# A graph layer on one core: the change of phases written as one table of steps by time, with the returned rows fetched behind the last piece of the table

## The chip, the cores and the metric

One Trainium2 chip, one of its cores. The metric is the device time of one execution in microseconds (us), median of the runs of a kernel. The engines of the core are TensorE (PE, matmuls), VectorE (DVE), ScalarE (ACT), GpSimd (POOL, here mostly the indirect gathers) and SyncE (SP, here the issuer of most transfers). Each works through its own instructions in order and waits on semaphores for the others.

## What is computed

6250 nodes of 256 features, 100000 edges sorted by destination, 16 relation types. In short form:

```
xn  = layernorm(x)
msg = (xn @ W[rel])[src] * edge_weight            # 16 relation matrices, 256 x 256
gnn = segment_sum(msg, dst)
q, k, v = xn @ Wqkv;  k = softmax(k, over all nodes)
ctx = k^T v per head (8 heads of 32);  out = q ctx
gate = sigmoid(gelu(ln(xn) @ Wg1 + bg1) @ Wg2 + bg2)
x   = x + gnn + (out * gate) @ Wproj + bproj
t   = layernorm(x);  top-2 of 8 experts by softmax(t @ router)
x   = x + t + sum_e weight_e * (gelu(t @ w1[e] + b1[e]) @ w2[e] + b2[e])
```

Matrices are split into a high and a low part (float32r), and a product is three passes (high·high, low·high, high·low).

## The kernel before

The nodes are 49 tiles of 128 (NT), processed as 24 pairs and one tile. **Phase one** goes over all tiles: keys, values and gate inputs, and the table of the 16 relation products, which is stored to memory in four pieces a tile; k and v rows go to `kv_d`. From tile 24 (K2) on it also gathers and sums part of the edges (3 of 8 edge tiles of a row of edges) and adds the contexts of the first 24 tiles. **Phase two** goes over the pairs `i` in eight slots `s` each, and the half group S = 8i + s of edges has 3 tiles for even s and 2 for odd s (`PART`). GpSimd gathers the tiles into a ring of six half groups (`gathers`: half group S waits until S − 6 is summed), and every engine has its share of a step:

- `SELECT` (DVE) makes the matrix of destinations; `MSGS` scales the gathered rows by the edge weight. For the first pairs (`WHOLE = 2`, half groups 0 to 15) ACT scales in place and PE sums in f32, two records a tile (`L2026`); later ACT writes a high part and DVE the low part (`L1611`), and PE sums both (`L2030`, `L2031`). `SUMS` (PE) adds up in a bank, `WINDOW`/`adds` (DVE, `L1625`) adds the bank to the nodes.
- For the pair one behind (`+`): `OUT`, `GATES`, `GATE_ACT`, `GATE`, `GATE_HI`, `GATE_LOW`, `PROJ`, `STATS` (which needs the first window of the next pair), `roots2` on POOL, `MEAN`, `NORM`, `TURN`, `TURN_HI`, `TURN_LOW`, `LOGIT`, `TOP`, and the first two layers of experts.
- For the pair two behind (`-`): `LAYER1 e` (PE, then gelu `L1090` and cast `L1095` on ACT, `LOW e` on DVE), `LAYER2 e`, `ADD e`, the weights of the two experts (`WEIGHT`, `COMB`...), the bias.

The order in each slot is written out by hand in `SLOTS_OF_PAIR`; an engine takes from it the steps it has. Pair 1 has its own list, `SLOTS_OF_SECOND`. In pair 0's slots only the steps of the edges apply, and other work is put between them by conditions on `(i, s)`:

- The first rows of phase two are 4 held k and v rows (`held_contexts`), then 21 rows that come back from `kv_d` in six parts of 4 and 3 (`load_rows` on SP, `shifts` on DVE `L1540`, `exps` on ACT `L996`, `contexts` on PE `L1982`), two parts in slot 0 and one in each of the slots 1 to 4 of pair 0. The two buffers are `slot` (7 rows) and `later` (14 rows).
- Slot 5: `finish_context` (DVE), `context_turn`, `context_values`; slot 6: `head_contexts`, `query_context`, `GATES 0`; slot 7: `query_high`, `query_low`, `OUT 0`.
- The expert weights come in four chunks of 2048 columns (n = 4 to 7), each cast on ACT (`split_hi`, `L847`) and subtracted on DVE (`split_lo`, `L1186`) at the places `SPLITS` and `SPLITS_LOW`; chunk n + 2 is loaded when chunk n is split.

For pair 0 PE takes `LAYER1 0` and `LAYER1 1` in slots 5 and 6 of pair 1 and the other layers in the slots of pair 2, so all of pair 1's sums stand before `LAYER1 2` and `LAYER2 0`.

A rare branch (`far > 0`, edges too far from their window) is not entered with this input; its flag is loaded into a register (`value_load`) on POOL, DVE and PE.

Of the kernel before, what the change touches and what calls it, by code (L numbers as in the profile page):

```python
# [38 lines left out]
def gps_layer(nc, x, src, dst, rel, norm, Wr, Wqkv, Wproj, bproj, ln_g, ln_b, Wg1, bg1, Wg2, bg2,  # L39
# [14 lines left out]
    ROOTS, FIRST_ROOTS = (7, 1), (5, 0)  # L54
# [30 lines left out]
    WC = 4  # L85
    AHEAD = 2 * X
# [21 lines left out]
    with ctx:  # L108
# [62 lines left out]
        ctxbd = sb("ctxbd", [P, CC, P], F32, two)  # L171
        hgp = sb("hgp", [2 * G, 2, P], F32R, two)
        dg = sb("dg", [P, C], F32, two)
# [10 lines left out]
        ct = sb("ct", [3 * CW, 2 * P], F32R, two)  # L184

# [87 lines left out]
        half = small[:, 38:40]  # L273
        vea = small[:, 64:64 + NT - K2]
# [214 lines left out]
        def _(sp):  # L489
# [44 lines left out]

            def load_kept(k, i):
# [78 lines left out]
        def _(pool):  # L614
# [28 lines left out]
            pool.wait_ge(consts, 10)  # L643
# [196 lines left out]
        def _(act):  # L840
# [157 lines left out]
            def beside(i, s):  # L998
# [7 lines left out]
                if (i, s) == (1, 4):  # L1006
                    act.wait_ge(w_lo, 8)
# [1247 lines left out]
```

## Time and profile before

| | |
|---|---|
| median of 3 runs | 1598.66 us (1596.49 to 1599.17) |
| the profiled execution | 1598.54 us, span 1596.7 us |
| PE busy | 1563.8 us (98%), 10509 matmul records |
| DVE, ACT, POOL busy | 1339.1, 962.8, 1021.2 us |
| mean granted clock | 0.995 |

The span is the time from the first to the last instruction. Busy time of PE is modelled from pipelined matmuls, so a busy PE need not be at its peak. Phase one ends near 721 us; pair 3's slots begin at 827.85 us.

### The profile page before, as it was taken

How to read it: one execution, taken by the hardware profiler on the slowest of the kernel's cores; microseconds unless marked ns; L12 is line 12 of the kernel's file. 1: busy time of each engine (PE TensorE's matmuls, PEld its weight loads, DVE VectorE, ACT ScalarE, POOL GpSimd, SP SyncE). 2: the span in 40 equal slices, each digit the busy share in tenths (PEclk: the TensorE clock that was granted, in tenths of full speed). 3: DMA queues.
4: the chain of work that ended last, by engine and by line, in shares of the span. 5: the costliest groups of instructions: out<-in, count | busy, mean ns of one | idle time of the engine just before them, and what ended most of it. 6: DMA issues, size and time to landing. Idle time of an engine off the chain costs nothing.

```text
span 1596.7 us, 31746 instructions
## 1 busy us (share of the span) xinstructions
PE 1563.8 (98%) x10509; PEld 1439.2 (90%) x10509; DVE 1339.1 (84%) x3389; ACT 962.8 (60%) x2156; POOL 1021.2 (64%) x1111
## 2 busy tenths in 40 slices
PE   7999999999999999998799999999999999999998
PEld 6888788888888888887699999999999999999998
DVE  7888656488888888884699999999999999999985
ACT  4455322356565665654677776777677777777764
POOL 4433222677777777757687777777777777767720
PEclk9999999999999999999999999999999999999999
DMA  9776665688888889889433333343333333333320
GB/s 301 264 256 242 243 237 226 231 291 272 277 278 279 283 283 284 277 261 317 144 111 108 116 109 108 112 113 104 103 117 107 110 106 109 112 105 113 107 53 10
DMA packets 127076, 290.50 MB, mean 182 GB/s; under 512 B 21271, under 2 KB 49724, under 8 KB 126914
## 3 DMA queue, kind: packets, MB, share of 16 engines
q1 hardware_dynamic: 86068, 177.19, 30.2%
q0 software_dynamic: 39952, 110.13, 26.3%
q8 instruction: 85, 1.39, 0.4%
q10 hardware_dynamic: 894, 1.16, 0.2%
q14 instruction: 77, 0.63, 0.1%
HBM read 149.49 MB, written 138.90 MB: 181 GB/s over the span
## 4 chain that ended last, share of the span: by engine, by line
PE 94%; DMA 1%; DVE 1%; issue 1%; ACT 1%; POOL 1%; ACTq 0%; SPq 0%; DVEq 0%; POOLq 0%
PE bank L1826 74%; PE bank L2030 4%; PE bank L2031 3%; PE bank L1870 2%; PE bank L1871 2%; PE bank L1982 1%; PE bank L1881 1%; PE bank L2026 1%; POOL raw L700 1%; DMA raw<-table,idxa 1%; PE bank L2068 1%; PE bank L2080 1%; PE bank L1836 1%; DMA pad<-in_L_mix_Wg 1%; PE bank L2077 1%
## 5 line engine op out<-in xcount | busy, mean ns | idle before, releaser
L818 POOL DMA_INDIRECT stg<-table,idxcur x495 | 546.7, 1104 | 145.1 <-issue 133.1
L1826 PE MATMUL bank<-wreg,xt 128*128 128x512 f32 x2352 | 579.1, 397 | 0.2
L1826 PEld LDWEIGHTS bank<-wreg,xt 128*128 128x128 f32 x2352 | 433.4, 189 | 88.0 <-ACT stg L864 1.0
L700 POOL DMA_INDIRECT raw<-table,idxa x297 | 306.6, 1032 | 87.7 <-issue 73.7
L1826 PE MATMUL bank<-tt,wreg 128*128 128x256 f32 (+1 forms) x2400 | 324.4, 284 | 0.0
L1826 PE MATMUL bank<-wreg,ht 128*128 128x256 f32 x2352 | 313.1, 282 | 0.2 <-DVE ht L1727 0.2
L1826 PEld LDWEIGHTS bank<-tt,wreg 128*128 128x128 f32 x2400 | 300.4, 189 | 2.5
L1826 PEld LDWEIGHTS bank<-wreg,ht 128*128 128x128 f32 x2352 | 292.1, 189 | 0.4 <-DVE ht L1727 0.4
L1090 ACT ACTIVATE raw<-bank,cols 128x256 f32<-128x256 f32 (+1 forms) x400 | 164.8, 463 | 101.4 <-PE bank L1826 101.0
L1611 DVE SCALAR_TENSOR_TENSOR ml<-stg,nrm,mh 128x256 fp32r<-128x256 f32 x455 | 195.2, 478 | 13.0 <-ACT mh L1034 13.0
L1034 ACT ACTIVATE mh<-stg,nrm 128x256 fp32r<-128x256 f32 x455 | 200.8, 499 | 0.0
L889 ACT ACTIVATE mh_a<-raw,nrm 128x256 fp32r<-128x256 f32 x297 | 129.6, 500 | 118.1 <-DMA raw<-table,idxa 117.8
L1228 DVE COPY stg<-bank 128x512 f32<-128x512 f32 x196 | 134.2, 686 | 75.5 <-PE bank L1826 74.5
L1741 DVE SCALAR_TENSOR_TENSOR xres<-bank,raw,xres 128x256 f32<-128x256 f32 x392 | 169.7, 473 | 13.1 <-PE bank L1826 11.4
L864 ACT COPY stg<-bank 128x512 f32<-128x512 f32 x196 | 112.5, 581 | 101.8 <-PE bank L1826 100.2
L1361 DVE SCALAR_TENSOR_TENSOR ml_a<-raw,nrm,mh_a 128x256 fp32r<-128x256 f32 x297 | 126.7, 480 | 53.0 <-ACT mh_a L889 52.5
L1095 ACT CAST ht<-raw 128x512 fp32r<-128x512 f32 (+1 forms) x200 | 122.5, 612 | 72.4 <-PE bank L1826 67.4
L1727 DVE TENSOR_TENSOR ht<-raw,ht 128x512 fp32r<-128x512 f32 (+1 forms) x200 | 134.6, 673 | 11.7 <-ACT ht L1095 9.5
L2030 PE MATMUL bank<-mh,sel 128*128 128x256 f32 x455 | 120.3, 291 | 0.0
L2031 PE MATMUL bank<-ml,sel 128*128 128x256 f32 x455 | 117.0, 281 | 0.0
L665 POOL TENSOR_TENSOR xres<-xres,bpb 128x256 f32<-128x256 f32 x24 | 19.4, 809 | 136.0 <-DVE kvs L1215 135.5
L1594 DVE TENSOR_TENSOR sel<-dbl,dpr 128x384 fp32r<-128x384 f32 x198 | 95.0, 480 | 9.7 <-PE bank L2026 9.6
(244 smaller groups left out, 2134.8 us busy)
## 6 DMA issues: line engine op xcount, KB each, us to landing
table<-stg SPq DMA_DIRECT2D x196, 512.0 KB, 3.9
kv_d<-kvs SPq DMA_DIRECT2D x49, 256.5 KB, 5.2
xt_d<-xt SPq DMA_DIRECT2D x49, 256.0 KB, 4.7
xtp<-xt_d SPq DMA_DIRECT2D x24, 512.0 KB
stg<-table,idxcur POOLq DMA_INDIRECT x495
sk<-kv_d SPq DMA_DIRECT2D x24, 256.5 KB, 5.7
out_x<-xres SPq DMA_DIRECT2D x24, 256.0 KB
xres<-in_x POOLq DMA_DIRECT2D x23, 256.0 KB, 4.2
```

Source lines behind the costliest of these rows:

```text
L700: pool.indirect_dma_start(ring_a[:, r * EARLY + j, :], None, table[0:LIMIT, :], bass.IndirectOffsetOnAxis(ap=idxa[:, at:at + 1], axis=0)). ...
L818: pool.indirect_dma_start(stg[:, ring_at(S, j), :], None, table, bass.IndirectOffsetOnAxis(ap=idxcur[:, at:at + 1], axis=0)).then_inc(gath ...
L889: act.activation(mh_a[:, (r % 2) * EARLY + j, :], ring_a[:, r * EARLY + j, :], ACT.Copy, scale=nrm[:, bass.ds(EB * q + j, 1)]).then_inc(hi ...
L1034: act.activation(mh[:, (s % 2) * CUT + j, :], stg[:, ring_at(S, j), :], ACT.Copy, scale=nrm[:, bass.ds(at + j, 1)]).then_inc(msg_hi, 1)
L1090: act.activation(hf[e % 2][:, c * 256:c * 256 + nt * P], bank[2 + e % 2][:, c * 256:c * 256 + nt * P], ACT.Gelu, bias=b1c[:, 2 * e + c:2 * ...
L1228: dve.tensor_copy(stage[:, j // 2, (j % 2) * 512:(j % 2 + 1) * 512], bank[3 + j % 4][:]).then_inc(copied(k, j)[0], 1)
L1611: dve.scalar_tensor_tensor(out=ml[:, m, :], in0=stg[:, ring_at(S, j), :], scalar=nrm[:, bass.ds(at + j, 1)], in1=halves(mh[:, m, :]), op0= ...
L1727: dve.tensor_tensor(ht[e % 2][:, LO, :, 0:n], cols2(hf[e % 2], n), halves(ht[e % 2][:, HI, :, 0:n]), ALU.subtract).then_inc(h_lo, 1)
L1741: dve.scalar_tensor_tensor(out=xk, in0=bank[6 + e % 2][:, a * C:(a + 1) * C], scalar=comb[:, a, e:e + 1], in1=xk, op0=ALU.mult, op1=ALU.ad ...
L1826: mm = pe.matmul(dst, stat(a, c), mov(b, c), start=(n == 0), stop=(n == 3 * chunks - 1))
L2030: pe.matmul(bank[u % 2][:, 0:C], sel[:, m, :], mh[:, m, :], start=(s % 2 == 0 and j == 0), stop=False)
L2031: mm = pe.matmul(bank[u % 2][:, 0:C], sel[:, m, :], ml[:, m, :], start=False, stop=(s % 2 == 1 and j == PART[1] - 1))
```

## The change

- The change of phases (pairs 0 to 2, half groups 0 to 23) is one list, `CHANGE`, followed by every engine with `follow`; the conditions on `(i, s)` and `SLOTS_OF_SECOND` are gone, and `run` begins at pair 3.
- Parts 2 to 5 of the returned rows stand earlier among the sums. SP's loads are written as two loops with single rows; parts 0 and 1 are shifted and exponentiated ahead of the wait for the end of phase one.
- Half groups 4 to 19 are whole in place of 0 to 15 (`WHOLE_GROUPS`).
- A chunk of expert weights is cast and subtracted in two halves (`HIGH n h`, `LOW_PART n h`).
- `NORM` is divided: the second scaling of the rows is the step `KEEP`, in `CHANGE` behind `TURN_HI` for pair 0.
- A tiny gelu (`GELU_TABLE`) stands between `MSGS 0 3` and `MSGS 0 4` on ACT.
- `LAYER1 2` and `LAYER2 0` of pair 0 stand before the sums of half group 13 (they stood behind 15); the rest of pair 0's experts is spread over half groups 13 to 23.
- GpSimd: the mask of heads has four columns and is made at the start; the roots of pairs 0 and 1 come before gather (4, 0) and (5, 1) of the next pair in place of (5, 0) and (7, 1).
- PE's load of the far flag and its branch stand behind two parts of rows, DVE's behind `SHIFT 1`.
- Some small buffers have places of their own instead of in `raw`.

```diff
-    ROOTS, FIRST_ROOTS = (7, 1), (5, 0)
+    ROOTS, EARLIER_ROOTS = (7, 1), {1: (4, 0), 2: (5, 1)}
...
-            load_rows(0)
-            load_rows(1)
-            first_phase_over(sp)
-            for part in range(2, 2 * GROUPS):
-                load_rows(part)
+            sp.wait_ge(sum_a, ER)
+            for b in range(2):
+                sp.wait_ge(kv_st[b], 16 * ((KEPT + SLOTS) // 2))
+            for n in range(FREE_ROWS):
+                load_row(n // 4, n)
+            sp.wait_ge(ctx1_mm, KEPT)
+            for n in range(FREE_ROWS, SLOTS):
+                load_row(1, n)
+            first_phase_over(sp)
+            for returned in range(2, 2 * GROUPS):
+                for n in range(*span_of(returned)):
+                    load_row(returned, n)
...
-                sp.wait_ge(w_lo, n + 1)
+                sp.wait_ge(w_lo, splits_of(n, 1))
                 load_chunk(n + 2)
...
+            def HIGH(n, h):
+                act.wait_ge(raw_in[n % 2], 32 * (n // 2 - 1))
+                if n >= 6:
                     act.wait_ge(ctx_mm, HELD + REST)
+                act.copy(wreg[:, HI, place_of(n), h * CC // 2].rearrange("p r o -> p (r o)"),
+                         raw[:, n % 2, h * WC * C:(h + 1) * WC * C]).then_inc(w_hi, 1)
...
+            for ready in range(2):
+                EXP(ready)
             first_phase_over(act)
...
-                act.wait_ge(edge_mm, S - 1)
+                if S < 2:
+                    act.wait_ge(ctx_mm, HELD)
+                else:
+                    act.wait_ge(edge_mm, S - 1)
...
+            def LOW_PART(n, h):
+                dve.wait_ge(w_hi, splits_of(n, h))
+                dve.tensor_tensor(wreg[:, LO, place_of(n), h * CC // 2].rearrange("p r o -> p (r o)"),
...
+            for ready in range(2):
+                SHIFT(ready)
+            dve.wait_ge(flag_ready, 1)
+            far = dve.value_load(flag[0:1, 0:1], min_val=0, max_val=NT * P * R)
+            first_phase_over(dve)
...
-WHOLE = 2
+WHOLE_GROUPS = (4, 20)
...
+CHANGE = (
+    "HELD_ROWS", "ROWS_OF 0", "ROWS_OF 1", "FAR_EDGES", "SELECT 0 0", "SELECT 0 1", "FADE", "SHIFT 2", "EXP 2", "SHIFT 3",
+    "MSGS 0 0", "ROWS_OF 2", "EXP 3", "SUMS 0 0", "ROWS_OF 3", "SHIFT 4", "MSGS 0 1", "EXP 4", "SELECT 0 2",
+    "ROWS_OF 4", "SUMS 0 1", "SHIFT 5", "EXP 5", "SELECT 0 3", "MSGS 0 2", "ADDS 0 0", "ROWS_OF 5", "MSGS 0 3", "GELU_TABLE",
+    "SUMS 0 2", "SUMS 0 3",
+
+    "CONTEXT", "SELECT 0 4", "MSGS 0 4", "SELECT 0 5", "CONTEXT_PE", "CONTEXT_TURN", "SUMS 0 4", "HIGH 4 0", "MSGS 0 5",
+    "VALUES", "ADDS 0 1", "LOW_PART 4 0", "HEADS", "SUMS 0 5", "HIGH 4 1", "HIGH 5 0", "SELECT 0 6", "QUERY", "GATES 0 2",
+    "LOW_PART 4 1", "QUERY_ROWS", "GATE_ACT 0 2", "OUT 0 2", "MSGS 0 6", "SELECT 0 7", "ADDS 0 2", "SUMS 0 6", "GATE 0 2",
+    "GATE_HI 0 2", "MSGS 0 7", "CLEAR", "GATE_LOW 0 2", "SUMS 0 7", "PROJ 0 2", "HIGH 5 1", "SELECT 1 0", "LOW_PART 5 0",
+    "MSGS 1 0", "ADDS 0 3", "SELECT 1 1", "SUMS 1 0", "LOW_PART 5 1", "MSGS 1 1", "SUMS 1 1", "SELECT 1 2", "ADDS 1 0",
+    "HIGH 6 0", "STATS 0 2", "LOW_PART 6 0", "MSGS 1 2", "SUMS 1 2", "MEAN 0 2", "NORM 0 2", "TURN 0 2", "SELECT 1 3",
+    "TURN_HI 0 2", "TURN_LOW 0 2", "KEEP 0 2", "MSGS 1 3", "SUMS 1 3", "LAYER1 0 2 0", "SELECT 1 4", "HIGH 6 1",
+    "LOGIT 0 2", "LOW_PART 6 1", "LAYER1 0 2 1", "ADDS 1 1", "MSGS 1 4", "TOP 0 2", "LOW 0 2 0", "SUMS 1 4", "HIGH 7 0",
+
+    "WEIGHT 0 2", "SELECT 1 5", "LOW 0 2 1", "MSGS 1 5", "COMB 0 2", "COMB_HI 0 2", "LAYER1 0 2 2", "LAYER2 0 2 0", "OUT 1 2",
+    "SUMS 1 5", "GATES 1 2", "LOW_PART 7 0", "SELECT 1 6", "ADDS 1 2", "HIGH 7 1",
...
+    "ADD 0 2 5", "LOW 0 2 7", "MSGS 2 3", "BIAS2_ADD 0 2", "TURN 1 2", "TURN_HI 1 2", "LAYER2 0 2 6", "SUMS 2 3",
+    "TURN_LOW 1 2", "ADDS 2 1", "SELECT 2 4", "MSGS 2 4", "SUMS 2 4",
+
+    "ADD 0 2 6", "LAYER1 1 2 0", "LOGIT 1 2", "SELECT 2 5", "MSGS 2 5", "LAYER2 0 2 7", "LOW 1 2 0", "TOP 1 2", "SUMS 2 5",
+    "LAYER1 1 2 1", "ADDS 2 2", "ADD 0 2 7", "SELECT 2 6", "MSGS 2 6", "SUMS 2 6", "SELECT 2 7", "MSGS 2 7", "SUMS 2 7",
 )
+def follow(order, **steps):
+    for entry in order:
+        name, *numbers = entry.split()
+        if name in steps:
+            steps[name](*map(int, numbers), *((8,) if name in OF_GROUPS else ()))
...
-    for i in range(2, pairs):
+    for i in range(3, pairs):
```

## Rows read from the trace of the kernel before

**Rows 1.** The page, busy us, share and instructions of each engine.

```profile
PE 1563.8 (98%) x10509; PEld 1439.2 (90%) x10509; DVE 1339.1 (84%) x3389; ACT 962.8 (60%) x2156; POOL 1021.2 (64%) x1111
```

**Rows 2.** Busy time in two windows: PE, PEld, DVE, ACT, POOL, clock, DMA.

```profile
720.00:827.85 107.85, 91.96 (x552) 81.94 (x550) 68.71 (x158) 62.26 (x124) 79.41 (x81) 0.94 0.61 195
827.85:860.70 32.85, 32.85 (x278) 32.72 (x277) 30.98 (x87) 23.69 (x56) 25.90 (x26) 1.00 0.41 113
```

**Rows 3.** Waits of PE, 715 to 800 us: total, times, longest.

```profile
PE bank L2026 <- ACT stg L1030: 4.1, 2, 2.6
PE bank L1982 <- ACT slot L996: 3.9, 1, 3.9
PE bank L2007 <- DVE ctxbd L1761: 1.6, 1, 1.6
...
PE bank L2068 <- ACT scr L1055: 1.2, 1, 1.2
```

**Rows 4.** Windows of 2 us on PE: busy, granted clock, DMA share, GB/s.

```profile
728.00:730.00 2.00, 0.00 (x0) 0.61 1.08 316
...
734.00:736.00 2.00, 2.00 (x8) 0.68 1.05 379
...
786.00:788.00 2.00, 0.66 (x2) 0.62 0.30 76
...
792.00:794.00 2.00, 1.97 (x6) 0.68 0.45 131
```

**Rows 5.** PE's timeline: start, us, line, operation, records, idle before.

```profile
730.03 8.90 PE L1982 MATMUL bank<-slot 128*128 128x257 f32 x28 [3.94 <-ACT slot L996]
...
749.16 6.23 PE L1982 MATMUL bank<-later 128*128 128x257 f32 x28
755.23 2.32 PE L2026 MATMUL bank<-stg,sel 128*128 128x256 f32 x10
...
782.14 1.78 PE L1826 MATMUL bank<-tt,wreg 128*128 128x256 f32 x12
...
796.39 1.58 PE L1826 MATMUL bank<-wreg,ht 128*128 128x256 f32 x12
```

**Rows 6.** PE's timeline at the start of pair 3's slots.

```profile
827.85 1.60 PE L1826 MATMUL bank<-tt,wreg 128*128 128x256 f32 x12
829.29 1.59 PE L1826 MATMUL bank<-wreg,ht 128*128 128x256 f32 x12
```

**Rows 7.** DVE's timeline: shift, weight subtraction, selection, low messages, window.

```profile
727.66 1.23 DVE L1540 TENSOR_TENSOR slot<-slot,dg 128x1024 f32<-128x1024 f32 x1 [3.46 <-DMA slot<-kv_d]
...
753.35 2.37 DVE L1186 TENSOR_TENSOR wreg<-raw,wreg 128x2048 fp32r<-128x2048 f32 x1 [2.36 <-ACT wreg L847]
...
820.12 0.55 DVE L1594 TENSOR_TENSOR sel<-dbl,dpr 128x384 fp32r<-128x384 f32 x1
...
821.85 1.27 DVE L1611 SCALAR_TENSOR_TENSOR ml<-stg,nrm,mh 128x256 fp32r<-128x256 f32 x3
...
823.75 0.88 DVE L1625 TENSOR_TENSOR xres<-bank,xres 64x256 f32<-64x256 f32 x2
```

**Rows 8.** ACT's timeline: weight cast, then the first gelu and messages.

```profile
751.44 1.88 ACT L847 CAST wreg<-raw 128x2048 fp32r<-128x2048 f32 x1
...
784.00 1.28 ACT L1090 ACT_TABLE_LOAD   x1 [2.39 <-PE bank L1826]
785.29 0.84 ACT L1090 ACTIVATE raw<-bank,cols 128x256 f32<-128x256 f32 x2
786.17 0.62 ACT L1095 CAST ht<-raw 128x512 fp32r<-128x512 f32 x1
786.69 2.10 ACT L1030 ACTIVATE stg<-stg,nrm 128x256 f32<-128x256 f32 x5
```

**Rows 9.** POOL's first gather of phase two; landing of the weight chunks.

```profile
725.00 0.99 POOL L818 DMA_INDIRECT stg<-table,idxcur  x1 [1.23 <-DMA table<-stg]
...
DMA to landing us min/median/max: 3.8/9.3/14.2
```

More of the change, by code:

```diff
@@ L797, in _ @@
                     pool.wait_ge(far_x, k + 1)
+            for h in range(PIECES):
+                pool.wait_ge(tbl_st[h], 16 * NT)
             def gathers(i, groups):
@@ L1097, in slot_of @@
             def slot_of(i, s, groups, p1, n1, p2, n2):
[L1098 to L1109 removed]
+                in_slot(i, s, groups, p1, n1, p2, n2, MSGS=MSGS, GATE_ACT=GATE_ACT, GATE_HI=GATE_HI, NORM=NORM, KEEP=KEEP,
+                        TURN_HI=TURN_HI, WEIGHT=WEIGHT, COMB_HI=COMB_HI, COMBT_ACT=COMBT_ACT, LAYER1=LAYER1)
+            follow(CHANGE, EXP=EXP, HIGH=HIGH, GELU_TABLE=GELU_TABLE, QUERY_ROWS=QUERY_ROWS, MSGS=MSGS,
+                   GATE_ACT=GATE_ACT, GATE_HI=GATE_HI, NORM=NORM, KEEP=KEEP, TURN_HI=TURN_HI, WEIGHT=WEIGHT, COMB_HI=COMB_HI,
+                   COMBT_ACT=COMBT_ACT, LAYER1=LAYER1)
             run(slot_of, NP, TAIL_GROUPS)
@@ L1625, in adds, with ADDS @@
                     dve.tensor_tensor(xk, bank[u % 2][a:b, 0:C], xk, ALU.add).then_inc(edge_add, 1)
+            def ADDS(i, u, groups):
+                adds(i, u)
             def WINDOW(i, s, groups):
@@ L1958, in _ @@
             pe.wait_ge(k_shift_diag, 2)
-            pe.matmul(bank[1][:, C:2 * C], halves(ones[:]), dg[:], start=True, stop=True).then_inc(kmb_mm, 1)
-            pe.wait_ge(flag_ready, 1)
-            far = pe.value_load(flag[0:1, 0:1], min_val=0, max_val=NT * P * R)
+            pe.matmul(bank[1][:, C:2 * C], halves(ones[:]), dg, start=True, stop=True).then_inc(kmb_mm, 1)
             pe.wait_ge(add_a, ALL_ADDS)
@@ L2179 @@
     ("-ADD 2", "*SELECT", "-LOW 4", "-COMBT_ACT", "*MSGS", "+STATS", "-LAYER1 5", "+PROJ", "-LAYER2 3", "*SUMS"),
-    ("-ADD 3", "*SELECT", "-LOW 5", "*MSGS", "+MEAN", "*WINDOW", "-LAYER1 6", "+NORM", "-LAYER2 4"),
+    ("-ADD 3", "*SELECT", "-LOW 5", "*MSGS", "+MEAN", "*WINDOW", "-LAYER1 6", "+NORM", "+KEEP", "-LAYER2 4"),
     ("-ADD 4", "*SELECT", "-LOW 6", "*MSGS", "*LAST_WINDOW", "-LAYER1 7", "*SUMS 4", "+TURN", "+TURN_HI", "-LAYER2 5", "*SUMS",
@@ L2186 @@
 )
-SLOTS_OF_SECOND = (
-    ("*SELECT", "*MSGS", "*WINDOW", "+GATE", "+GATE_HI", "+GATE_LOW", "*SUMS"),
-    ("*SELECT", "*MSGS", "+PROJ", "*SUMS"),
-    ("*SELECT", "*MSGS", "*WINDOW", "+STATS", "*SUMS"),
-    ("*SELECT", "*MSGS", "+MEAN", "+NORM", "*SUMS"),
-    ("*SELECT", "*WINDOW", "+TURN", "+TURN_HI", "*MSGS", "+TURN_LOW", "*SUMS"),
-    ("*SELECT", "+LAYER1 0", "+LOGIT", "*MSGS", "*LAST_WINDOW", "+LOW 0", "*SUMS"),
-    ("*SELECT", "+TOP", "*MSGS", "*WINDOW", "+LAYER1 1", "*SUMS"),
-    ("*SELECT", "*MSGS", "*SUMS"),
-)
+OF_GROUPS = ("SELECT", "MSGS", "SUMS", "ADDS")
+CHANGE = (
+    "HELD_ROWS", "ROWS_OF 0", "ROWS_OF 1", "FAR_EDGES", "SELECT 0 0", "SELECT 0 1", "FADE", "SHIFT 2", "EXP 2", "SHIFT 3",
[26 rows of a table added]
+)
+def follow(order, **steps):
[3 more added lines that the diff above has]
+            steps[name](*map(int, numbers), *((8,) if name in OF_GROUPS else ()))
 def in_slot(i, s, groups, p1, n1, p2, n2, **steps):
-    for entry in (SLOTS_OF_SECOND if isinstance(i, int) and i == 1 else SLOTS_OF_PAIR)[s]:
+    for entry in SLOTS_OF_PAIR[s]:
         name, *expert = entry[1:].split()
```

232 lines of the change are left out of this document (92 added, 140 removed), and 9 rows, old and new, of the table CHANGE.

## The prediction

> **What bounds the kernel now.** I read the page first. TensorE (PE) is busy in 98% of the span and is nearly the whole chain that ended last [rows 1]. The list of waits by engine names no PE wait at all from 800 to 1500 us. The windows by stage say the same: from 827.85 us (the first layer-1 product of pair 3's slots) one pair of tiles takes 32.85 us, PE busy in all of it, VectorE (DVE) in 30.98, ScalarE (ACT) in 23.69 [rows 2]. So neither end of the kernel is in play, and an edit counts only by what PE loses in the change of phases, 720 to 827.85 us, where it is busy 91.96 of 107.85 us. The steps that the diff reorders all lie there.
>
> The list of PE's waits there adds up to the 15.9 us (four of its ten rows stand in [rows 3]): 3.9 for the first returned rows, then nine short ones between 757 and 787 us, each the latency of one link of pair 0's first passage (context, query, gate, projection, norm, turn, first expert). Two stretches of low clock come on top [rows 4]: granted 0.50, the lower of the two levels (1.2 GHz), after the wait at 726 and again after the one that ended at 787, each some 6.5 us. The first costs 2.7 us (28 records of returned rows in 8.90 us against 6.23 later [rows 5]). The second is full of work except 0.6 us, so it costs about 3.0.
>
> PE's work up to 827.85 is the same in both kernels: as many rows, products and message tiles. Sixteen half groups have whole (f32) messages in both; they are groups 0 to 15 before and 4 to 19 after. So I walk the new table with durations of these rows and ask when PE reaches the same place.
>
> **The walk.** Durations, start to start: a whole tile 0.43 on PE (5 in 2.16), a split tile 0.24, a returned row 0.87 (28 records are 7 rows in 6.1 [rows 5]), an expert layer 1.42 [rows 6]. On DVE a selection 0.35 to 0.47, a low message 0.42, a window 0.35 to 0.8, a weight subtraction 2.3 and so 1.15 for a half [rows 7]. On ACT a message 0.42, a gelu with its cast 1.45, an expert weight cast 1.9 and so 0.95 for a half [rows 8].
>
> Up to 738.8 nothing moves: the rows are issued at the same place behind the last store of the table, and PE's first row waits for the same landing. Then the new order puts the rows of the returned parts ahead of the sums, and of the sums only groups 0 and 1 (5 split tiles, 1.2 us) stand before the last row, where four whole half groups (10 tiles, 4.3 us) stood. The last row ends at 752.1 in place of 755.2: **3.1 earlier**.
>
> From there the chain, each end worked out from the one before: context sums on DVE 753.3 (the low messages of group 3 are ahead of them), its turn on PE 754.0, copy 755.0 (two selections ahead), VALUES 756.4, HEADS 757.1, QUERY 758.3, its two halves 759.7, OUT 761.5, the gate's three steps 763.7, PROJ 765.8, groups 8 and 9 on PE 767.9, one window 768.8, STATS 770.9 (2.1, as in the trace), roots and MEAN 772.4, NORM and TURN 774.2. KEEP is now behind TURN_HI, and halves of weights pass between, so the chain is stopped less than by the 2.3 us pieces of before. But then ACT does KEEP (1.0) and MSGS 1 3, and PE has SUMS 1 3 ahead of LAYER1 0: it starts at 777.1, where it was 782.1 [rows 5]. PE idles 1.0 at QUERY_ROWS, 1.3 elsewhere, 4.2 before TURN, 2.0 behind it.
>
> Next LAYER1 0, LOGIT, LAYER1 1 end at 781.1. The gelu table load, 1.28 us on the path at 784.0 before [rows 8], now lies near 750, where ACT waits for DVE anyway. MSGS 1 4 is behind HIGH 6 1 and two gelus, so PE idles 2.2. LAYER2 0 starts at 785.7. Before it was 796.4 [rows 5], but with groups 13 to 15 summed (7 whole tiles, 3.0) and without the dearer sums of 16 to 19 still ahead (10 tiles, 1.9): comparable is 791.5. **Lead 5.8 us** at full clock.
>
> **The clock.** A wait of 4.2 us, followed by 0.6 us of transposes and 2.0 more of waiting, is longer than either that brought the low clock before [rows 3, 4]. I expect one stretch of 6.5 us that begins between 773 and 777: 1.5 us lost if it is early, 3.3 if it holds work throughout; I take 2.3. Lead 3.5. The Trainium skill has the same picture (TensorE: Matmul & The Clock Gate, What's actually happening): throttled is the default and activity releases it; the trace agrees with 0.50 and 1.00, and by that rule, too, the wait of 4.2 us ends in the low clock.
>
> **The tail gives it back.** Pair 0's experts now run beside groups 13 to 23, eleven in place of eight, so the last four groups of pair 2 stand close together, and these have split messages. Up to the end of SUMS 2 3 PE has 28.4 us of work after 785.7 and no wait in my walk. Then:
> - SUMS 2 4 directly follows SUMS 2 3, but its low messages are behind ADDS 2 1, which waits for SUMS 2 3: 0.4 window, 0.5 selection, three messages 1.3, less 0.5 of overlap: **1.7 idle**;
> - MSGS 2 5 is behind the gelu of LAYER1 1 0: **0.4**;
> - SUMS 2 6 directly follows LAYER1 1 1, but its messages on ACT are behind that layer's gelu (1.5), then message and low message, three tiles: **2.9**;
> - SUMS 2 7 behind it: **0.7**.
> Sum 5.7. The steady slots have none of these waits: they put the messages ahead of the layer. Result: 3.5 − 5.7 = **2.2 us slower**, place for place 830 in place of 827.85. The profiled execution took 1598.54 us for its span of 1596.7, the median is 1598.66, so 1600.9. As a check by idle time: 3.9 + 2.3 + 6.2 + 2.2 + 5.7 = 20.3 after against 15.9, and a low stretch of 2.3 against 3.0: +3.7. The two ways differ by 1.5 us, the drain of a matmul counted as busy or not; that is my error in any case.
>
> **Costed at nothing, with its cover.** POOL's head mask, three short operations, goes from 722 to the start and to four columns. POOL waits for DVE's first variance there, and PE then for a DMA; at 725 POOL waited 1.2 more for the table's store [rows 9], so nothing is won either. Without cover it is that 1.2 at most. The load of the far flag and its branch move on DVE between SHIFT 1 and SHIFT 2; before they lay inside a wait of 3.46 [rows 7], which bounds them. Of the gap of 2.9 us there 1.2 is free after two selections and FADE, and EXP 2 has 1.7 more before PE asks for it. So the loss is between 0 and 0.6; I take 0. The Trainium skill prices a compare-and-branch at about 0.1 us (Advanced Engine Details and Errata, Control Flow Timing); by that the sum stays as it is, and no row here times one. PE passes its branch with matmuls queued to 738.9. Chunk 6 of the weights leaves SP after LOW_PART 4 1, at 758.7 and not 755.7. These transfers took 3.8 to 14.2 us to land [rows 9]; at 5.3 it is there at 764, needed at 767; at 14.2 it would hold MSGS 1 2 and cost 2. GpSimd's gathers, 1.25 apart, wait for group 1's sum until 749.5 now and for STATS before group 12, and still land ahead of the messages that use them. The new small buffers cost nothing: only addresses change.
>
> **Rivals.**
> 1. *The tail hides* (chance 0.18). DVE and ACT are well ahead at SUMS 2 3 and the last groups cost PE little. For it: DVE is 1 to 2 us idle in several slots of the walk. Against it: the orders above are fixed by waits, not by load. If at most 1.5 of 5.7 are lost, the kernel is faster by 2 to 5.8: 1593 to 1596.6, say 1594.9. It turns faster from the point where the tail takes less than the lead, 3.5 us.
> 2. *A second low clock in the tail* (0.27). 2.9 and 0.7 idle with 0.7 of small sums between is near what preceded the stretch at 786.8. It would run into saturated slots and cost 2 to 3.3: 1603.5.
> 3. *No low clock near 775, or the table changes little* (0.15): lead 5.8, tail 5.7: 1598.6.
> The forecast itself has 0.40.
>
> **Numbers.** Likeliest 1600.9. A measurement here can tell 0.2% (3.2 us) from no change. Faster by more than that is nearly all of rival 1: 0.18. Slower is rival 2 and a quarter of the forecast: 0.37. Within it the rest: 0.45. The range takes in rival 1's middle and rival 2 with the 2 us of a late chunk: 1594.5 to 1605.5.
>
> **What would show it.** The windows should have PE idle 19 to 21 us up to pair 3 instead of 15.9; its waits should be for ACT and DVE messages late in the table (about 2.9 once, 1.7 once) and about 4 before TURN; returned rows should end near 752; a stretch at 0.50 should begin between 773 and 777, and layer 1 of expert 0 start near 777. If the first layer of pair 3's slots starts before 825, the tail was wrong; if LAYER2 0 starts after 790, the chain was; if PE waits for a DMA of weights, the chunks were.

## The result and the profile after

| | before | after |
|---|---|---|
| median (lowest to highest) | 1598.66 us (1596.49 to 1599.18) | 1605.69 us (1602.70 to 1609.76) |
| profiled execution, its span | 1598.54, 1596.7 | 1605.69, 1604.0 |
| mean granted clock | 0.995 | 0.993 |

The ratio is 1.0051, 95% interval 1.0038 to 1.0063: slower, by 7.0 us between the medians (the ratio stands for 8.2) where 2.2 was forecast, and 0.2 us above the top of the range. These seven runs of the changed kernel lie 7 us apart and the seven of the kernel before 3, but that can't be laid to the change: 28 later runs of the kernel before lie 9 us apart.

Phase one of this execution ended a little earlier: DVE's last copy of the table starts at 719.40, before at 720.15. In the other kernels timed below, which run the same phase one but for the change, it starts anywhere from 717.02 to 721.10, so a difference of 0.75 says nothing of the change. The tables below therefore count from that copy. From it to the first layer of pair 3's slots it was 107.70 us and is now 114.81: **7.1 us**. What of that goes to waits is in the list of PE's waits of the changed kernel from 715 to 834.3 us (total, times, longest), which answers to [rows 3]:

```profile
PE bank L2083 <- ACT scr L1068: 6.4, 2, 4.9
PE bank L2039 <- ACT stg L1040: 4.9, 3, 2.2
PE bank L1995 <- ACT slot L1004: 4.8, 1, 4.8
PE bank L2043 <- DVE ml L1628: 4.7, 4, 2.6
PE bank L1841 <- DVE wqc L1795: 1.0, 1, 1.0
```

They sum to 21.8 us, where the same list summed to 15.6 from copy to pair 3 before. Many short waits have become few long ones: before no wait in the passage of pair 0 was over 2.6, now there are 4.9, 2.15 and 2.1 in a row, one of 1.5 before the second turn, and four in the tail (2.6 the longest, 4.7 together), a place where before there was none. PE's timeline of the changed kernel has each (start, duration, records, idle before), answering to [rows 5] and [rows 6]:

```profile
729.99 8.36 PE L1995 MATMUL bank<-slot 128*128 128x257 f32 x28 [4.81 <-ACT slot L1004]
...
751.33 0.47 PE L2043 MATMUL bank<-mh,sel 128*128 128x256 f32 x1
...
774.20 1.11 PE L2083 MATMUL bank<-ident,scr 128*128 128x128 f32 x4 [4.92 <-ACT scr L1068]
777.47 2.05 PE L2039 MATMUL bank<-stg,sel 128*128 128x256 f32 x4 [2.15 <-ACT stg L1040]
778.95 3.10 PE L1841 MATMUL bank<-tt,wreg 128*128 128x256 f32 x12
...
786.48 1.53 PE L2039 MATMUL bank<-stg,sel 128*128 128x256 f32 x6 [2.08 <-ACT stg L1040]
787.66 1.77 PE L1841 MATMUL bank<-tt,wreg 128*128 128x256 f32 x12
789.27 1.58 PE L1841 MATMUL bank<-wreg,ht 128*128 128x256 f32 x12
790.68 1.59 PE L1841 MATMUL bank<-xtp,wqc 128*128 128x256 f32 x12
...
817.16 0.66 PE L2083 MATMUL bank<-ident,scr 128*128 128x128 f32 x4 [1.52 <-ACT scr L1068]
...
821.59 0.36 PE L2043 MATMUL bank<-mh,sel 128*128 128x256 f32 x1 [1.47 <-DVE ml L1628]
...
831.69 0.35 PE L2043 MATMUL bank<-mh,sel 128*128 128x256 f32 x1 [2.60 <-DVE ml L1628]
...
834.21 2.62 PE L1841 MATMUL bank<-tt,wreg 128*128 128x256 f32 x12
836.67 1.57 PE L1841 MATMUL bank<-wreg,ht 128*128 128x256 f32 x12
```

The first layer of an expert takes 3.10 us at 778.95 and some 1.6 elsewhere: the clock. Its windows (2 us each: PE busy, granted clock, DMA share, GB/s), answering to [rows 4]:

```profile
770.00:772.00 2.00, 0.00 (x0) 0.92 1.09 377
...
776.00:778.00 2.00, 0.53 (x1) 0.50 0.42 125
...
780.00:782.00 2.00, 2.00 (x12) 0.52 0.40 119
...
832.00:834.00 2.00, 1.68 (x10) 0.78 0.58 169
834.00:836.00 2.00, 2.00 (x11) 0.50 0.21 66
836.00:838.00 2.00, 2.00 (x17) 0.87 0.44 131
```

So the clock is at its lower level (1.2 GHz) for some 10 us around the first turn and for some 3.4 around 834: the half microsecond from 832.50 still has 1.00, the one from 833.50 has 0.50. Behind 838 both kernels run the same slots.

One wait of the tail can be followed over two engines. ACT's timeline of the changed kernel: the messages of `SUMS 2 6` (five of `L1047`) stand behind the gelu of the layer that PE has only just finished.

```profile
829.12 0.84 ACT L1106 ACTIVATE wv<-bank,cols 128x256 f32<-128x256 f32 x2 [2.55 <-PE bank L1841]
829.99 0.62 ACT L1111 CAST ht<-wv 128x512 fp32r<-128x512 f32 x1
830.52 2.10 ACT L1047 ACTIVATE mh<-stg,nrm 128x256 fp32r<-128x256 f32 x5
```

ACT was idle 2.55 us ahead of that gelu; its list has no message in that place.

### The profile page after: what moved, and what is told of

Same layout as the page of the kernel before. It is cut to its first block, busy times and chain, and to the rows that moved or that the text cites. A ratio compares the mean times of both kernels' runs of the same rounds, so it can differ in the third digit from the quotient of the medians.

```text
span 1604.0 us, 31756 instructions
## 1 busy us (share of the span) xinstructions
PE 1563.7 (97%) x10509; PEld 1439.3 (90%) x10509; DVE 1338.9 (83%) x3393; ACT 963.3 (60%) x2161; POOL 1028.4 (64%) x1111
## 4 chain that ended last, share of the span: by engine, by line
PE 92%; POOL 2%; DMA 2%; issue 2%; ACT 1%; DVE 1%; ACTq 0%; SPq 0%; DVEq 0%; POOLq 0%
PE bank L1841 73%; PE bank L2043 4%; PE bank L2044 3%; PE bank L1885 2%; PE bank L1886 2%; POOL raw L722 2%; PE bank L1995 1%; PE bank L1896 1%; PE bank L2039 1%; DMA raw<-table,idxa 1%; PE bank L2083 1%; PE bank L2095 1%; PE bank L1851 1%; DMA pad<-in_L_mix_Wg 1%; PE bank L2092 0%
## 5 line engine op out<-in xcount | busy, mean ns | idle before, releaser
L1047 ACT ACTIVATE mh<-stg,nrm 128x256 fp32r<-128x256 f32 x455 | 200.7, 499 | 2.9 <-PE bank L2044 2.9
L1761 DVE SCALAR_TENSOR_TENSOR xres<-bank,mix,xres 128x256 f32<-128x256 f32 x392 | 169.7, 473 | 18.1 <-PE bank L1841 16.4
L1106 ACT ACTIVATE wv<-bank,cols 128x256 f32<-128x256 f32 (+1 forms) x200 | 82.4, 464 | 62.3 <-PE bank L1841 62.3
L1106 ACT ACTIVATE cd<-bank,cols 128x256 f32<-128x256 f32 (+1 forms) x200 | 82.5, 463 | 46.4 <-PE bank L1841 46.1
L1111 ACT CAST ht<-wv 128x512 fp32r<-128x512 f32 (+1 forms) x100 | 61.2, 612 | 55.7 <-PE bank L1841 53.5
```

Of the source, the lines that this page charges most:

```text
L1047: act.activation(mh[:, (s % 2) * CUT + j, :], stg[:, ring_at(S, j), :], ACT.Copy, scale=nrm[:, bass.ds(at + j, 1)]).then_inc(msg_hi, 1)
L1106: act.activation(hf[e % 2][:, c * 256:c * 256 + nt * P], bank[2 + e % 2][:, c * 256:c * 256 + nt * P], ACT.Gelu, bias=b1c[:, 2 * e + c:2 * ...
L1761: dve.scalar_tensor_tensor(out=xk, in0=bank[6 + e % 2][:, a * C:(a + 1) * C], scalar=comb[:, a, e:e + 1], in1=xk, op0=ALU.mult, op1=ALU.ad ...
```

## The experiments

Eleven kernels ran, each timed in five rounds beside the kernel before. Two numbers are given for each: the ratio to the kernel before with its 95% interval, and the distance from the last table copy to pair 3's first layer in its one profiled execution (before 107.70, after 114.81). "Low clock" is the time at the lower level within that distance, added up over windows of 1 us as (1 − granted clock) / 0.5, and "waits" is the sum of PE's waits in it.

The last two columns say how far that one execution stands for its kernel: its own time less the kernel's median, and the granted clock as the mean of all timed executions. In a span of 1600 us each 0.001 of it is 3.2 us at the lower level.

| kernel | ratio [interval] | distance | waits | low clock | profiled less median | granted clock, mean of all |
|---|---|---|---|---|---|---|
| before | 1 | 107.70 | 15.6 | 13.6 | -0.1 | 0.9950 to 0.9952 |
| after | 1.0051 [1.0038, 1.0063] | 114.81 | 21.8 | 18.1 | 0.0 | 0.9929 |
| tail order | 1.0010 [0.9999, 1.0021] | 109.91 | 17.4 | 17.1 | +2.4 | 0.9944 |
| one sum earlier | 1.0042 [1.0025, 1.0059] | 118.55 | 20.4 | 27.3 | +6.0 | 0.9921 |
| pair 2 by the old slots | 1.0020 [1.0008, 1.0033] | 116.17 | 18.9 | 30.7 | +4.0 | 0.9929 |
| dummy work at the turn | 1.0029 [1.0016, 1.0042] | 113.23 | 16.3 | 7.9 | +0.4 | 0.9961 |
| tail, norm, dummy work | 0.9993 [0.9982, 1.0005] | 105.72 | 10.5 | 6.8 | +1.9 | 0.9976 |
| before with dummy work | 0.9992 [0.9981, 1.0003] | 107.06 | 14.0 | 10.3 | +0.2 | 0.9958 |
| groups 20 to 23 whole | 1.0035 [1.0022, 1.0048] | 113.64 | 20.3 | 17.1 | +2.3 | 0.9950 |
| tail, norm, two sums earlier | 1.0005 [0.9991, 1.0019] | 108.71 | 15.1 | 17.1 | -0.4 | 0.9935 |
| tail, norm | 1.0004 [0.9991, 1.0017] | 112.50 | 16.2 | 23.9 | +3.4 | 0.9942 |
| tail, norm, dummy work twice | 0.9983 [0.9970, 0.9995] | 104.06 | 7.0 | 0.0 | +0.8 | 0.9992 |
| before with dummy work twice | 0.9987 [0.9974, 1.0000] | 108.04 | 10.9 | 10.2 | +0.3 | 0.9967 |

### The tail's order

```diff
-    "ADD 0 2 5", "LOW 0 2 7", "MSGS 2 3", "BIAS2_ADD 0 2", "TURN 1 2", "TURN_HI 1 2", "LAYER2 0 2 6", "SUMS 2 3",
-    "TURN_LOW 1 2", "ADDS 2 1", "SELECT 2 4", "MSGS 2 4", "SUMS 2 4",
...
-    "ADD 0 2 6", "LAYER1 1 2 0", "LOGIT 1 2", "SELECT 2 5", "MSGS 2 5", "LAYER2 0 2 7", "LOW 1 2 0", "TOP 1 2", "SUMS 2 5",
-    "LAYER1 1 2 1", "ADDS 2 2", "ADD 0 2 7", "SELECT 2 6", "MSGS 2 6", "SUMS 2 6", "SELECT 2 7", "MSGS 2 7", "SUMS 2 7",
+    "ADD 0 2 5", "LOW 0 2 7", "MSGS 2 3", "BIAS2_ADD 0 2", "SELECT 2 4", "MSGS 2 4", "TURN 1 2", "TURN_HI 1 2",
+    "LAYER2 0 2 6", "SUMS 2 3", "TURN_LOW 1 2", "SUMS 2 4", "ADDS 2 1",
...
+    "ADD 0 2 6", "SELECT 2 5", "MSGS 2 5", "LAYER1 1 2 0", "LOGIT 1 2", "LAYER2 0 2 7", "SUMS 2 5", "SELECT 2 6", "MSGS 2 6",
+    "SELECT 2 7", "MSGS 2 7", "LOW 1 2 0", "TOP 1 2", "LAYER1 1 2 1", "ADDS 2 2", "ADD 0 2 7", "SUMS 2 6", "SUMS 2 7",
```

> The changed kernel with one edit: the last four half groups' selections and messages stand ahead of the windows and gelus that held them (SELECT and MSGS 2 4 ahead of TURN 1, MSGS 2 5 ahead of LAYER1 1 0, MSGS 2 6 and 2 7 ahead of LAYER1 1 1); PE's order is the same. Theory A, the order in the tail: PE waited 4.7 us there (1.5, 0.3, 2.6, 0.3) and then worked about 3.4 us at the low clock, 1.9 us lost. At least 3.5 of the idle and all of the low clock go, so 4 to 6.5 us faster than the changed kernel, near 1600. Theory B, the loss is the middle (wait before TURN 0 and the long low clock there): under 1 us. Theory C, the tail is short of DVE time whatever the order: the waits move to the windows, 0 to 2 us.

1599.12 us. The waits for low messages are gone from the list (4.7 to 0), and so is the low clock around 834; the waits ahead of both turns stay at 6.4, and so does the low clock in the middle. PE's order is the same, so this is a matter of where DVE and ACT do their share. It gives back 4.9 us of distance, and 1.0 more behind it, since pair 3's first layer is at full clock again; the ratios give 6.6 us (1.0051 to 1.0010, times 1598.7). It is the largest part of the loss.

### One sum ahead of the mean

```diff
-    ... "SUMS 1 2", "MEAN 0 2", "NORM 0 2", "TURN 0 2", "SELECT 1 3", "TURN_HI 0 2", "TURN_LOW 0 2", "KEEP 0 2", "MSGS 1 3", "SUMS 1 3",
+    ... "SUMS 1 2", "SELECT 1 3", "MSGS 1 3", "SUMS 1 3", "MEAN 0 2", "NORM 0 2", "TURN 0 2", "TURN_HI 0 2", "TURN_LOW 0 2", "KEEP 0 2",
```

> The changed kernel with one edit: SELECT, MSGS and SUMS 1 3 stand ahead of MEAN 0 in place of behind KEEP 0, so half group 11 is summed in the wait for TURN 0 and LAYER1 0 follows TURN_LOW. Theory B: the 2.15 us wait behind KEEP goes, and the sum (2 us at the low clock) leaves the low stretch: LAYER1 0 starts 2.5 to 3.5 us earlier, and the kernel is faster by 2 to 3.5 us. Theory A holds beside it, and its tail waits stay as they are (4.7 us). If the gathers are late for half group 11, PE waits for ACT on a DMA there and the gain is under 1 us.

1603.5 us, no clear gain, and the profile is worse in the middle. The 4.9 us ahead of the first turn are gone (the 1.5 left is the second turn's), but others have come: 4.0 for messages and 2.1 for a selection, and the low clock lasts 20 us, 772 to 793. PE's waits in this kernel, copy to pair 3:

```profile
PE bank L2039 <- ACT stg L1040: 4.7, 2, 4.0
PE bank L2043 <- DVE ml L1628: 4.7, 4, 2.6
PE bank L2039 <- DVE sel L1611: 2.1, 1, 2.1
PE bank L2083 <- ACT scr L1068: 1.5, 1, 1.5
```

The messages were late because ACT waited for the gathered rows of that half group; its timeline in this kernel:

```profile
772.64 0.91 ACT L1040 ACTIVATE stg<-stg,nrm 128x256 f32<-128x256 f32 x2 [4.21 <-DMA stg<-table,idxcur]
```

The wait was moved, not filled: that is the last case of what was expected. The profiled execution is 6 us slower than this kernel's median, so its 20 us of low clock are more than is usual for it; the mean granted clock of all its executions (0.9921) is still the lowest of the table.

### Pair 2 by its old slots

The table ends behind `SUMS 1 7`; `run` begins at pair 2, and its roots stand before gather (7, 1).

```diff
-    for i in range(3, pairs):
+    for i in range(2, pairs):
```

> The changed kernel with the table ended behind SUMS 1 7 and pair 2 run by the old slots, its roots at gather (7, 1); all sums of pair 1 stand before LAYER1 0 2 again, as in the kernel before. Theory A (the experts' spread over half groups 13 to 23 makes the tail): no PE wait in pair 2's slots, so the tail's 4.7 us and its low clock go, and so does the 1.5 us before TURN 1; 5 to 8 us faster than the changed kernel, near or under the kernel before. Theory B: the middle's loss stays, 10 us of low clock, and the kernel is no better than 2 us faster than the changed one.

1601.75 us. No wait for low messages is left, but the low clock comes twice, 773 to 787 and 790 to 801, in an execution 4 us slower than the median. So the old order of pair 2 gives back 5.0 us (1.0051 to 1.0020), and in this profile part of what it saves goes to the clock. As the expert layers stand elsewhere in this kernel, its distance is not to be read against the others'.

### Dummy work at the first turn

9 matmuls ahead of `TURN 0` and 4 behind it, into a bank that nothing reads.

```diff
+            def WARM(times):
+                for _ in range(times):
+                    pe.matmul(bank[7][:, 0:C], ident[:], dbl[:], start=True, stop=True)
...
-    ... "NORM 0 2", "TURN 0 2", "SELECT 1 3",
+    ... "NORM 0 2", "WARM 9", "TURN 0 2", "WARM 4", "SELECT 1 3",
```

> The changed kernel with extra matmuls whose result is never read: nine of 128x256 in f32 on PE in the wait before TURN 0, four in the wait behind it. They should fill 3.9 of 4.9 us and 1.7 of 2.1. If the low clock comes from these waits, the stretch at 0.50 (10.2 us) is gone, half group 11, the two first layers and the transposes take half their time, 2.5 to 3.5 us of work given back, and the kernel is 2 to 3.5 us faster though it does more. If the low clock is not due to these waits, it stays and the kernel is equal or up to 1 us slower. The tail's low clock stays in both cases.

1602.39 us, as forecast. The granted clock is 1.00 from 736 to 828, though PE still waits there, as two windows of this kernel show; the low clock of the tail, at 829, stays:

```profile
780.00:782.00 2.00, 0.95 (x8) 1.00 0.47 131
782.00:784.00 2.00, 0.96 (x5) 1.00 0.31 82
...
830.00:832.00 2.00, 2.00 (x10) 0.50 0.29 88
```

`LAYER2 0` starts 68.28 us behind the copy in place of 69.87: 1.6 us is what it gives back in this profile, and the ratios give 3.5 (1.0051 to 1.0029, with intervals that overlap a little). Over all executions the mean granted clock rose from 0.9929 to 0.9961, some 10 us less at the lower level, so the effect is not that of one profile.

### The three together

The tail's order, the dummy work, and the second normalisation ahead of the last cast of pair 0:

```diff
-    ... "MSGS 2 2", "LAYER1 0 2 7", "SUMS 2 2", "LAYER2 0 2 5", "MEAN 1 2", "NORM 1 2", "KEEP 1 2",
+    ... "MSGS 2 2", "MEAN 1 2", "NORM 1 2", "LAYER1 0 2 7", "SUMS 2 2", "LAYER2 0 2 5", "KEEP 1 2",
```

> The changed kernel with three edits at once: the messages and selections of the last four half groups ahead of windows and gelus, the second normalisation of pair 0 ahead of the cast of its first expert, and dummy matmuls of 128 x 256 around the first turn (9 before, 4 behind) into a bank of their own. Theory A (three separate losses: 4.7 us of waits in the tail with the low clock behind them, 1.5 us before the second turn, and a clock that is low for some 10 us at the first turns): they add up, no low clock behind 736, no wait over 1 us for the messages nor before the second turn; from the last table copy to pair 3 some 107 us or less; ratio to the kernel before 0.997 to 0.999 (1594 to 1597 us). Rival B (one loss hides another: the time goes to a wait elsewhere): the pair 3 distance stays at 109 to 110 and the ratio at 1.000 to 1.002, as in the run with the tail alone.

1596.66 us: as forecast in the profile (105.72; PE's waits for `L2083` 6.4 to 1.0, for the low messages 4.7 to 0.2, no low clock behind 736). The ratio of 0.9993 is at the upper edge of what was expected and can't be told from 1. One wait of 2.1 us for messages is left, before `SUMS 1 4`, where none over 1 us was expected; it is that of the changed kernel. The losses add up as far as can be told: 9.1 us of distance are gone against the changed kernel, and 9.3 by the ratios, where the tail order alone gave 6.6 and the dummy work alone 3.5.

### The kernel before, with dummy work behind the logits

```diff
                 mm.then_inc(logit_mm, 1)
+                if at_first(p):
+                    for _ in range(5):
+                        pe.matmul(bank[7][:, 0:C], ident[:], dbl[:], start=True, stop=True)
```

> The kernel before with 5 dummy matmuls of 128 x 256 behind the logits of pair 0, in the place where TensorE waits ahead of the low clock of 786.8 to 793. Theory A (the clock falls there because of the sparse work around that wait, as in the changed kernel): the low stretch is gone, pair 3 starts 2 to 3.3 us earlier, ratio 0.998 to 0.999. Rival B (the low clock comes whatever TensorE does there, or comes a little later): the same length of low clock at another place, ratio 1.000 or above by the work added (up to 1 us).

1596.2 us, not told apart from the kernel before. From the dummy matmuls on the clock stays full, and the wait of 2.6 us is 0.4. But this execution has a stretch of 6.8 us at 777 to 783, around the turn, and that lies ahead of the dummy work:

```profile
776.75 1.11 PE L2072 MATMUL bank<-ident,scr 128*128 128x128 f32 x4 [1.22 <-ACT scr L1059]
779.04 2.90 PE L2030 MATMUL bank<-stg,sel 128*128 128x256 f32 x6 [1.18 <-ACT stg L1034]
781.38 2.72 PE L1830 MATMUL bank<-tt,wreg 128*128 128x256 f32 x12
...
784.75 2.40 PE L2089 MATMUL bank<-dbl,ident 128*128 128x256 f32 x10
```

So the dummy work can't have moved the stretch there. Up to the turn this kernel does what the kernel before does, with the same waits (1.49, 1.47 and 1.22 us here, 1.50, 1.47 and 1.21 there), and one execution has the low clock and the other has not. The window of 776 to 778, of this kernel and then of the kernel before:

```profile
776.00:778.00 2.00, 1.11 (x4) 0.65 0.21 66
...
776.00:778.00 2.00, 1.13 (x4) 1.00 0.00 0
```

At its own place the dummy work did what theory A says, but pair 3 starts only 0.6 us earlier where 2 to 3.3 were expected: in this execution part of the gain went to the other stretch. Over all executions the mean granted clock is 0.9958 against 0.9950, some 2.6 us less at the lower level; the ratio leaves open whether that is a gain.

### Groups 20 to 23 whole

The sums of four more groups are made from unsplit messages; nothing is left out.

```diff
-WHOLE_GROUPS = (4, 20)
+WHOLE_GROUPS = (4, 24)
```

> The changed kernel with groups 20 to 23 multiplied whole in float32, as groups 4 to 19 are, so that no low part of their messages is made on DVE; their sums are more exact, nothing is left out. Theory A (the tail waits because the chain gelu, message, low part of the message is longer than a half group's matmuls now that nothing else stands between them): the waits for the low messages of the last groups go, 4.7 us, and the low clock behind them with its 1.9; TensorE's own work grows by some 2 us: ratio to before 1.001 to 1.003, between the run with the tail alone and the changed kernel, pair 3 at 111 to 112 us from the last table copy (114.8 in the changed kernel). Rival B (the wait is for the gelu or the gathered rows, and the low message is only the last link): waits of like size stand before the sums, now for the message, and the time is 2 us above the changed kernel's, ratio 1.006.

1603.13 us, ratio and distance between those of the two theories. The low messages are gone from PE's waits, but waits for the messages themselves and for a selection stand in their place, 2.08 and 1.03 us in the tail:

```profile
823.03 1.53 PE L2039 MATMUL bank<-stg,sel 128*128 128x256 f32 x6 [1.03 <-DVE sel L1611]
...
832.69 2.40 PE L2039 MATMUL bank<-stg,sel 128*128 128x256 f32 x10 [2.08 <-ACT stg L1040]
```

So of the 2.60 us ahead of `SUMS 2 6` the last link, the low message, is worth some 0.5; the other 2.1 are the place of the messages behind the gelu. No low clock came in this tail.

### Order alone, with two sums ahead

The tail, the normalisation, and `SUMS 1 3` and `SUMS 1 4` with their selections and messages ahead of `MEAN 0`; the roots of pair 0 back ahead of gather (5, 0).

> The changed kernel reordered without dummy work: the messages and selections of the last four half groups ahead of windows and gelus, the second normalisation of pair 0 ahead of the cast of its first expert, the sums of half groups 3 and 4 of the first two groups of this stage ahead of the means and the first turn, and the roots of pair 0 behind the sixth half group as in the kernel before. Theory A: no wait in the tail, none before the second turn, and two half groups of matmuls more between the logits and the first turn, so that the waits there shrink from 10 us to some 4; the low clock stays only if the work there is still sparse. Pair 3 at 107 to 109 us from the last table copy; ratio 0.998 to 1.000. Rival B (the sums moved ahead wait for their own gathers, as in the run that moved one of them): low clock of 10 us or more and pair 3 at 110 us or later, ratio 1.001 to 1.004.

1598.57 us. Waits for sums in the middle again (2.9 and 1.3, then 2.2 for `ht` before `LAYER2 0`), low clock for 6.8 us from 770 and 3.4 from 787. As with one sum, ACT waited for gathered rows there (5.7 us before the messages of `SUMS 1 4`). The kernel can't be told apart from the kernel before: rival B in the trace, theory A in the time.

### Tail and normalisation alone, and dummy work at both places

> The changed kernel with the tail's order (messages and selections of the last four half groups ahead of windows and gelus) and the second normalisation of pair 0 ahead of the cast of its first expert; no dummy work. It shows what the two orders give without the dummy matmuls of the run that had all three. Theory A (the losses add up): the wait before the second turn (1.5 us) goes and the one of the tail (4.7) stays away, the low clock of some 10 us at the first turns stays; from the last table copy to pair 3 some 108.4 us (109.9 with the tail alone), ratio 0.999 to 1.001. Rival B (the second turn's wait was hidden in another): 109.5 us or more, ratio as with the tail alone, 1.001.

1598.83 us. The second turn's wait is gone (`L2083` 4.9, once), the tail's too. But this execution had the low clock for 14 us in the middle, and for 3.4 more from 789, and its distance (112.50) lies above that of the tail alone. The ratios are 1.0004 and 1.0010, not told apart, and the mean granted clock of all executions is 0.9942 and 0.9944, so this profile has more low clock than is usual for its kernel. One profile does not carry a difference of 2 us where the low clock takes part.

```diff
-    "HELD_ROWS", "ROWS_OF 0",
+    "HELD_ROWS", "WARM 9 4", "ROWS_OF 0",
```

(9 dummy matmuls into bank 4, while PE waits for the first returned rows.)

> As the run with the two orders and the dummy matmuls around the first turn, and 9 more dummy matmuls of 128 x 256 behind the matmuls of the held rows, where TensorE waits 4.9 us for the first returned rows and the clock is low for some 7 us behind. Theory A (sparse work brings that low clock too): the low stretch of 728 to 735 goes and with it some 3 us; from the last table copy to pair 3 some 102.5 us, ratio 0.997 to 0.998, faster than both kernels. Rival B (the clock falls there whatever TensorE does, or the rows of this stage land no earlier than they are used, so that a faster clock only lengthens a wait): 105 us or more, ratio 0.999 or above.

1595.44 us, ratio 0.9983 [0.9970, 0.9995]: the fastest kernel measured here. No window between copy and pair 3 is under full clock, and PE waits 7.0 us in all. The returned rows now run at full speed (28 records in 6.33 us in place of 8.36) and soon wait for the next:

```profile
725.46 4.05 PE L2160 MATMUL bank<-dbl,ident 128*128 128x256 f32 x18
730.17 6.33 PE L1995 MATMUL bank<-slot 128*128 128x257 f32 x28 [0.66 <-ACT slot L1004]
737.23 3.74 PE L1995 MATMUL bank<-later 128*128 128x257 f32 x16 [0.72 <-ACT later L1004]
```

The distance shrank by 1.7 us, not by the 3 expected; 0.7 of the difference is this new wait.

> The kernel before with the dummy matmuls behind the logits of pair 0 and 9 more behind the matmuls of the held rows. It is what the new order has to beat. Theory A: the low stretch of 728 to 734 goes, some 3 us, and pair 3 starts some 104 us behind the last table copy (107.1 in the run with the first dummies alone), ratio 0.997 to 0.998; the changed kernel with both kinds of dummy work and the two orders is 1 to 2 us faster than this one. Rival B: as for that one, 106.5 us or more and 0.999 or above.

1596.7 us, 0.9987 [0.9974, 1.0000]. The low clock of 728 is gone here too, but there is one of some 3 us at 757, and again one of some 7 at 777, ahead of the dummy work behind the logits. The distance of 108.04 is that of rival B, the ratio lies between the theories. One profile can't say whether the stretch at 757 has to do with the dummy work: no other kept trace has it. The two kernels with both kinds of dummy work can't be told apart by their ratios.

## Why the prediction was off, step by step

The walk in the same places, in us from the last table copy (predicted times less 720.15, measured less 719.40):

| place | predicted | measured | difference added |
|---|---|---|---|
| end of the returned rows | 31.95 | 31.93 | 0 |
| TURN 0 | 54.05 | 54.80 | +0.75 |
| LAYER2 0, low clock included | 67.85 | 69.87 | +1.3 |
| end of SUMS 2 3 | 96.25 | 100.72 | +2.45 |
| pair 3's first layer | 109.85 | 114.81 | +0.5 |

- **The rows and the chain: right.** Rows end 3.1 us earlier relative to the copy, as said. PE idles 1.02 at `QUERY_ROWS`, 4.92 before the turn, 2.15 behind it and 2.08 before `SUMS 1 4`; said were 1.0, 4.2, 2.0 and 2.2. The first returned row came 0.7 us later behind the copy (a wait of 4.81 against 3.9), for which no cause was found. It is the kernel and not the execution: without dummy work in that place the wait is 4.8 to 5.1 in the changed kernel and all its variants, and 3.9 in the kernel before and its variant. The rows are issued 1.19 us behind the copy in both, and landed after a median of 4.9 us in place of 4.5. The rows behind it made it up, and the turn is then 0.75 late by small differences of the chain.
- **"One stretch of 6.5 us that begins between 773 and 777": mis-sized.** It began near 771.7 and lasted 10 us, so that all of `LAYER1 0` lay in it (3.10 us instead of 1.6). The step took the length from the stretches of before. There PE was full of work from 787.34 on, here it had 0.53 us of work in the window 776 to 778; that this made the stretch longer is likely but not shown.
- **"28.4 us of work after 785.7 and no wait in my walk": this step failed.** It measured 30.85, 789.27 to 820.12. 1.5 of it is the second turn: `NORM 1` stood on ACT behind the cast of the last expert, which waits until PE has read its buffer; with the two exchanged the wait was gone (6.4 to 4.9 for `L2083` in the kernel with both orders, 1.0 with the dummy work). The other 0.9 is work: counted over at the walk's own prices (14 layers, 17 whole tiles, 1.6 us of small products) it is 28.8, so 0.4 was left out of the count, and 0.5 is records that took longer than their price. ACT's records of the cast and of `NORM 1` in the changed kernel:

```profile
815.50 0.62 ACT L1111 CAST ht<-wv 128x512 fp32r<-128x512 f32 x1 [1.69 <-PE bank L1841]
816.02 1.09 ACT L1068 ACTIVATE scr<-xres,small 128x256 f32<-128x256 f32 x2
```

- **The tail: mechanism right, 4.7 us of waits instead of 5.7** (1.47, 0.28, 2.60, 0.32 for 1.7, 0.4, 2.9, 0.7), shown by the order alone: it takes them away, and the kernel is 6.6 us faster.
- **Rival 2 came true with it, at 1.5 us and not at 2 to 3.3.** The low clock from 833.1 on makes the four records ahead of 834.21 some 0.5 us dearer (0.99 in place of 0.48) and pair 3's first layer 1.0 (2.46 from start to start in place of 1.44). With that last 1.0, place for place, the loss is 7.1 + 1.0 = 8.1, and the profiled executions say the same: 7.3 us of span and 0.75 of the earlier copy. The forecast had the tail's waits and left the clock to a rival; the two belong together, as the tail order shows: with the waits the low clock is gone. With the four whole groups it is gone too, though PE still waits 2.08.
- **What was costed at nothing** cost nothing visible: PE waits for no weights, flag or mask.
- **There was a lead at LAYER2 0, by estimate**: 69.87 against 71.35 (the 791.5 of the prediction, itself worked out and not measured, less 720.15), 1.5 us ahead of before at a comparable place where 3.5 were forecast. From there to pair 3 the kernel before takes 36.35 us by the same estimate and the changed one 44.94: the 8.6 lost are 1.5 at the second turn, 4.7 of waits in the tail, 0.5 of its clock and 1.9 left over. About 1.0 of the 1.9 is in the records right behind the tail's waits, at full clock: the six at 821.59 take 1.04 us and the six at 831.69 take 1.21, where six take 0.72 without a wait. The rest has no shown cause.

Of the 5.9 us that the loss (8.1) lies above the forecast, 0.75 had come by the turn, 1.3 came around it, 2.45 in the stretch costed at 28.4, 0.5 in the tail and 1.0 in pair 3's first layer. No one step holds the whole miss.

The Trainium skill (TensorE: Matmul & The Clock Gate, What's actually happening) has activity as what releases the throttle. The runs agree: dummy work at the first turn removed the low clock there in all three kernels that had it, and in the two variants of the kernel before none stands right behind the dummy matmuls either.

What stays open: why the first returned row lands later, why the low stretch in the middle was 10 us long in one kernel and 14 in another with nearly the same waits around it, why the same waits brought it at 777 in one execution and not in another, and 0.9 us of dearer work.

## What to carry to other kernels

When steps of several tiles are written as one list, read it engine by engine: a message that stands behind a gelu or a window waits for PE, and PE then waits for it. When an order packs waits together, put the price of the low clock into the forecast itself, not into a rival. In these traces every wait of 2.6 us and more that held no dummy work was followed by the lower level, waits of 2.1 and 2.2 in some kernels and not in others, and a run of waits none above 1.5 in two executions and not in a third; so it is a chance with a price, here 1.5 to 3 us a stretch. And a place that has just come free is only worth moving work to if that work's gathers are there: moving a sum ahead of the mean only changed what PE waited for.

## What the runs showed that was not expected

- With the granted clock at 1.00, twelve records of an expert layer take 1.61 us from start to start right behind the f32 sums (787.66 to 789.27) and 1.41 behind another layer (789.27 to 790.68). This is not all a cost: three tiles of sums between two layers take 1.10 us (796.31 to 797.41) where the price of 0.43 a tile gives 1.29. Sums and the layer behind them together are between 0 and 0.2 us dearer than their prices.
- Work that does nothing can shorten a kernel: 22 dummy matmuls in three waits and the reordering brought the changed kernel from 1605.69 to 1595.44 us, while the reordering alone gave 1598.83.
- The low clock isn't tied to one wait, nor to the kernel: behind the same waits one execution has it and another has not. Two stretches behind the same first wait of 3.9 us differ as well, 6.8 us long in the profile of the kernel before and 3.4 in that of its variant with dummy work behind the logits, which comes later. What one profile shows of it should be set beside the mean granted clock of all executions.
